# A perceiver block in fp32 on one core: the score order turned, the clip bound by way of DRAM, 76 padded first maxima

## The reference

```
x = x + xattn(layernorm(x), ctx_768, ...)   # x: (4, 256, 256), ctx_768: (4, 4096, 192)
x = x + attn(layernorm(x), ...)
x = x + ffn(layernorm(x), ...)

def xattn(query, key_value, ...):           # 16 heads of width 16
    q, k, v = query @ Wq + bq, key_value @ Wk + bk, key_value @ Wv + bv   # split into heads
    attn = clip(einsum('bhqd,bhkd->bhqk', q, k) * D ** -0.5, -10000, 10000)
    return softmax(attn) @ v @ Wo + bo
```

## Time and profile before

| | us |
|---|---|
| median of 3 runs | 1135.63 (1135.35 to 1148.06) |
| the profiled execution, whole | 1132.47 |
| its span, first to last instruction | 1130.7 |
| PE busy | 1043.2 |
| DVE busy | 825.7 |
| ACT busy | 712.5 |
| POOL busy | 380.7 |

### The profile page before, as it was taken

One profiled execution on the slowest core, in us unless ns is written; L12 is line 12 of the kernel. 1 busy time (PEld: TensorE's weight loads), 2 busy tenths in 40 slices (PEclk: granted clock), 3 DMA queues, 4 the chain that ended last, 5 costly groups with the idle time before them and its releaser, 6 DMA issues.

```text
span 1130.7 us, 29261 instructions
## 1 busy us (share of the span) xinstructions
PE 1043.2 (92%) x11521; PEld 718.0 (63%) x11521; DVE 825.7 (73%) x1549; ACT 712.5 (63%) x1382; POOL 380.7 (34%) x440
## 2 busy tenths in 40 slices
PE   7899797999999999999999999999999888978997
PEld 6687575767767676766767676655555454646655
DVE  7566686889888888888888888878878223693553
ACT  2222476777787777877877787767777654405342
POOL 5733445445444544444445442040000000203320
PEclk9899599999999999999999999979999899999999
DMA  7854653546455554555545454224431100000001
GB/s 218 236 170 136 186 167 104 173 137 169 141 165 156 145 154 144 168 148 145 167 136 162 142 162 113 61 70 117 136 99 43 30 2 2 1 1 2 3 1 38
DMA packets 117137, 128.56 MB, mean 114 GB/s; under 512 B 20007, under 2 KB 91370, under 8 KB 116970
## 3 DMA queue, kind: packets, MB, share of 16 engines
q1 hardware_dynamic: 111498, 120.20, 36.6%
q10 hardware_dynamic: 5472, 6.23, 2.1%
HBM read 88.61 MB, written 37.75 MB: 112 GB/s over the span
## 4 chain that ended last, share of the span: by engine, by line
PE 76%; issue 7%; DVE 7%; ACT 7%; DMA 1%; POOL 1%; SPq 1%; ACTq 0%; POOLq 0%; DVEq 0%
PE acc L1794 21%; PE st L1754 16%; PE mx L1740 9%; PE kps L1702 8%; PE misc L1740 5%; DVE free_k L1436 2%; PE st L1598 2%; ACT prob L994 2%; ACT qst L906 1%; PE mx L1736 1%; PE setB L2053 1%; ACT prob L1082 1%; DVE mxp L1189 1%; PE acc L1598 1%; PE mx L1593 1%
## 5 line engine op out<-in xcount | busy, mean ns | idle before, releaser
L1189 DVE TENSOR_REDUCE mxp<-mx 128x1 f32<-128x512 f32 x709 | 466.5, 683 | 106.4 <-PE mx L1740 71.3
L994 ACT ACTIVATE prob<-st 128x512 f32<-128x512 f32 x704 | 377.1, 600 | 152.7 <-PE st L1754 152.2
L1754 PE MATMUL st<-qst,kst 51*128 51x256 f32 x2048 | 409.9, 311 | 31.5 <-ACT qst L906 22.4
L1754 PEld LDWEIGHTS st<-qst,kst 51*128 51x128 f32 x2048 | 299.4, 190 | 66.9 <-ACT qst L906 25.5
L1740 PE MATMUL mx<-kst,qst 51*128 51x512 f32 x645 | 267.8, 436 | 1.8 <-DVE mxp L1189 1.5
L1189 DVE TENSOR_REDUCE mxp<-misc 128x1 f32<-128x512 f32 x315 | 215.0, 682 | 36.7 <-PE misc L1740 35.8
L994 ACT ACTIVATE xn<-st 128x512 f32<-128x512 f32 x320 | 172.2, 600 | 56.8 <-PE st L1754 56.4
L1794 PE MATMUL acc<-prob,v_raw 128*17 128x256 f32 x2816 | 193.9, 394 | 9.2 <-issue 5.4
L1740 PEld LDWEIGHTS mx<-kst,qst 51*128 51x128 f32 x645 | 122.9, 191 | 69.1 <-issue 35.9
L1740 PE MATMUL misc<-kst,qst 51*128 51x512 f32 x315 | 135.6, 430 | 0.0
L1702 PE MATMUL kps<-ctx_p,w_hi 64*128 64x256 f32 x528 | 129.2, 311 | 4.9 <-POOL ctx_p L717 4.9
(11 more groups left out here) (429 smaller groups left out, 1285.0 us busy)
## 6 DMA issues: line engine op xcount, KB each, us to landing
kst<-kscr SPq DMA_DIRECT2D x240, 128.0 KB, 2.5
kscr<-kraw SPq DMA_DIRECT2D x100, 256.0 KB, 2.7
kst<-kscr SPq DMA_DIRECT2D x240, 64.0 KB, 2.6
ctx<-in_ctxT SPq DMA_DIRECT2D x93, 128.0 KB, 2.7
ctx<-in_ctxT SPq DMA_DIRECT2D x184, 64.0 KB, 2.4
kscr<-prob SPq DMA_DIRECT2D x16, 256.0 KB, 4.6
kscr<-o_sb SPq DMA_DIRECT2D x12, 256.0 KB, 4.0
qscr<-v_raw SPq DMA_DIRECT2D x8, 256.0 KB, 2.5
```

Source lines behind the costliest of these rows:

```text
L994: act.activation(exps(unit_at(n)), st_bank("scores", unit_at(n))[:, :], ACT.Exp).then_inc(exp_done, 1)
L1189: dve.reduce_max(at, bank_of_max(n)[:, :], AX.X).then_inc(max_red, 1)
L1754: mm = pe.matmul(st_bank("scores", n)[:, h * T:(h + 1) * T], kst[row, j // 2, at:at + P], qst[row, 2 * (q % 3) + j // 2, :], start=True, s ...
```

## The change

- **The order in a step.** The step's last score, unit n+3, moves behind `values` and so to the next step's start, where its halves alternate with those of the next score. Maxima come one pass later, the fourth one ahead of three passes and of score n+1. The heads of the maxima go 0, 2, 1, 3 in place of 1, 0, 2, 3.
- **The bound** `low` is no longer made by TensorE and ScalarE in full: ScalarE takes the exponential of the 128x8 shift (`low_bound`, once a group), SP writes these 1024 numbers to DRAM and reads them back onto all partitions. The two matmuls and two activations of each group go, and their two places among the score banks.
- **The first 76 maxima** are all padded (`qz2`, in the memory of `xn`, holds group 1's queries), and three of four are followed by a piece of projection.
- **The shift** has its place among the score banks, and its copy on ScalarE, at t = 58.
- **VectorE** makes the low parts of the weights, behind its 76 reductions; GpSimd splits the first context chunk ahead of key chunk 19. VectorE's copy of the second half of a value chunk comes at t % 8 = 5, ScalarE's copies at t % 4 = 0.
- **GpSimd** adds the first output bias in four parts behind groups 1 to 4, not at once behind group 0.

```diff
-                    if more:
-                        max_unit(n + AHEAD)
-                    score_half(n, 0)
-                    score_half(n, 1)
-                    next(some, None)
...
-                    score_half(n + 3, 0)
-                    next(some, None)
-                    score_half(n + 3, 1)
-                    next(some, None)
+                    if n:
+                        score_half(n - 1, 0)
+                    score_half(n, 0)
+                    if n:
+                        score_half(n - 1, 1)
+                    score_half(n, 1)
+                    next(some, None)
                     if more:
+                        max_unit(n + AHEAD)
...
+                    for h in range(2):
+                        score_half(n + 2, h)
+                    for _ in range(2):
+                        next(some, None)
                     if more:
                         max_unit(n + 3 + AHEAD)
-                    next(some, None)
-                    next(some, None)
-                if t == 3:
-                    for e in range(2):
-                        spread_low(q, e)
+                    for _ in range(3):
+                        next(some, None)
+                    for h in range(2):
+                        score_half(n + 1, h)
...
+            def write_low(q):
+                sp.wait_ge(low_col, q + 1)
+                with nc.allow_non_contiguous_dma("1024 bounds from columns to a row"):
+                    sp.dma_start(lscr[q].rearrange("(j n p) -> p j n", j=4, n=QT), lowc[:, :, :]).then_inc(low_set, 16)
+            def read_low(q):
+                sp.wait_ge(low_set, 32 * q + 16)
+                wait(sp, clip_done, UQ * q)
+                sp.dma_start(low[:, :, :].rearrange("p j t -> p (j t)"),
+                             lscr[q].rearrange("(o n) -> o n", o=1).to_broadcast([P, 4 * T])).then_inc(low_set, 16)
...
-                act.activation(low_pairs[:, :, e, :], st_bank("low", 2 * q + e)[:, :].rearrange("p (i t) -> p i t", i=2),
-                               ACT.Exp, bias=negclip[:, :]).then_inc(low_set, 1)
+                act.activation(lowc[:, :, :], shift[:, :, :], ACT.Exp, bias=negclip[:, :],
+                               scale=-1.0).then_inc(low_col, 1)
...
-            return m - m // 6 + F0 if m % 6 < 5 else None
+            return m - m // 4 + F0 if m % 4 < 3 else None
...
+            for raw, hi, lo in weights:
+                dve.tensor_tensor(lo, raw, hi.bitcast(F32), ALU.subtract).then_inc(w_lo_set, 1)
...
-                if q == 0:
+                if 1 <= q <= 4:
                     pool.wait_ge(bo_in, 32)
-                    add_bias(0)
-                    pool.wait_ge(x_bias, 4)
+                    add_bias(0, (q - 1,))
+                    pool.wait_ge(x_bias, q)
```

More of the change, by code:

```diff
@@ L113, in build @@
         low = sb("low", [P, 4, T])
-        low_pairs = low[:, :, :].rearrange("p (i e) t -> p i e t", e=2)
         accs = sb("accs", [P, T])
@@ L382, in build @@
             st_users.append(("scores", unit_at(n)))
-            if t == 3:
-                st_users += [("low", 2 * q), ("low", 2 * q + 1)]
-            if t == 59 and q + 1 < NQ:
+            if t == 58 and q + 1 < NQ:
                 st_users.append(("shift", q + 1))
@@ L591, in _ @@
                     sp.wait_ge(st_ps, UQ * q + 8 * k + 8)
+                    if k == 7 and q + 1 < NQ:
+                        write_low(q + 1)
                     if 8 * q + k + RB < 8 * NQ:
@@ L673, in q_split, with add_bias @@
                 pool.tensor_tensor(q_sb[:, :, cols], q_sb[:, :, cols], q1[:, :, cols], ALU.subtract).then_inc(q_2, 1)
-            def add_bias(k):
+            def add_bias(k, parts=range(4)):
                 pool.wait_ge(ln_xn, NT * (k + 1))
-                for n in range(4):
+                for n in parts:
                     xs = x_sb[:, 2 * n:2 * n + 2, :]
@@ L1006, in _ @@
                         v_copy_half(c, 0)
-                if t == 60 and q + 1 < NQ:
+                if t == 57 and q + 1 < NQ:
+                    low_bound(q + 1)
+                if t == 58 and q + 1 < NQ:
                     shift_rows(q + 1)
@@ L1151, in ones_rows @@
                 for r in (32, 96):
-                    dve.memset(kst[r:r + 32, :, first * 512:end * 512].bitcast(F32), 1.0).then_inc(ones_set, 1)
+                    dve.memset(kst[r:r + 32, :, first * 512:end * 512].bitcast(F32), 1.0).then_inc(rows_set, 1)
             def norm_part(first, end):
@@ L1345, in _ @@
                     reduce_unit(n + AHEAD)
-                if t % 8 == 6 and v_job(q, t // 8) is not None:
+                if t % 8 == 5 and v_job(q, t // 8) is not None:
                     v_copy_half(v_job(q, t // 8))
@@ L1944, in _ @@
                         slot_products(at)
+            for h in range(2):
+                score_half(NU - 1, h)
             values(NQ - 1, 15)
```

124 lines of the change are left out of this document (61 added, 63 removed).

## The result

| | median of the runs | profiled run | its span | granted clock |
|---|---|---|---|---|
| before | 1139.8 us (1135.4 to 1148.1, 4 runs) | 1132.5 | 1130.7 | 0.967 |
| after | 1368.6 us (1353.5 to 1377.6, 4 runs) | 1372.3 | 1370.5 | 0.896 |

The account below looks back on a forecast made before the run. Bound: a chain through ScalarE and three score banks, not TensorE's work. Prologue -9, group 0 -2.3, groups 1 to 10 +33, 11 to 13 +5.3, 14 +2.3, 15 +0.7: together +30, 1165 us by the median's measure, range 1138 to 1192.

Parts of the forecast that it names:

- prologue: Before the first values: VectorE makes the low weights, first pass at 119.6, first values about 125; -9 us (-5 to -12).
- groups 1 to 10: Main groups: each 2.8 us longer at 53.1, plus 5 for the bias quarters; +33 us in all.
- groups 11 to 13: Late groups: from 153.0 us to 158.3, with steps of 3.16 and 2.2 a group at the seams; +5.3 us.
- The other ring: Three banks of maxima in each step: the fourth waits for the first's reduction until 1.50; step 3.16 against 2.885 us.
- the first rival: In each step the fourth maximum finds its bank free, TensorE's work bounds, steps of 2.80, 1075 us; chance 9%.
- From group to group: Seam costs over sixteen plain steps: shift 1.1, transpose 0.2, GpSimd 0.5, clock 0.3; a group 53.1 us, +2.8.
- The bias: Quarters behind groups 1 to 4 show in full, four times 1.25 us, against 5.4 saved behind group 0; nothing won.
- The bound by DRAM: Write of 1024 elements and 512 KB read, 16 times: costed at nothing, block loads late if the write took over 9 us.
- the seams gave nothing back: Rival between groups: no shift wait, no half clock, GpSimd in time, steps at 3.10; 1144 or 1136 us; chance 13%.
- no load was pulled ahead of a waiting one: Rival in each step: the held maximum's weights load during its wait, saving 0.115 us, 1138 us; chance 6%.
- Pauses of 0.2 us in each step: Rival on TensorE's clock: pauses of 0.3 to 0.5 us in each step lower it, 31 us more, 1196; chance 6%.
- the sign named for being wrong: In the main groups: value blocks 2.8 us apart, or a clock under 1.00 mid group, would refute the forecast.

Follow-up runs that it names:

- without the trip: The changed kernel with neither the write of the 1024 bounds to DRAM nor the 512 KB read back; 1194.5 us, ratio to before 1.050.
- run 7: The changed kernel without the DRAM write and read, first maximum at the step's head, fourth behind score n+1; 1146.1 us, ratio to before 1.009.
- run 9: The changed kernel without the DRAM write and read, old step order and places, bias in one piece behind group 0; 1134.0 us in one run.
- run 2: The changed kernel with the bound's DRAM write and read issued in the middle of its group; 1304.4 us, ratio to before 1.148.
- run 12: The changed kernel without the bound's DRAM write and read, SP's writes of K chunks 16 to 18 moved earlier; 1191.5 us.
- run 6: The kernel before plus an unread write per seam of 1024 four-byte elements, each 64 bytes from the next in DRAM; 1140.9 us in one run.
- run 5: The kernel before plus an unread 4 KB write per seam, 32 bytes in one piece per partition; 1139.9 us, ratio to before 1.002.

## Why the prediction was right and wrong

The span grew by 239.8 us: 174.3 by the trip, 65.5 by the rest (without the trip against before, profiled runs). The second part against the prediction's own terms (one profile against one, so the first row can be off by some 3 us and the last by 5: behind the last values all these kernels take anything from 181 to 187):

| term | forecast | without the trip |
|---|---|---|
| prologue | -9 | +6.8 (first values 140.98 against 134.15) |
| group 0 | -2.3 | -1.3 |
| groups 1 to 10 | +33 | +49.8 |
| groups 11 to 13 | +5.3 | +2.2 |
| groups 14, 15 | +3.0 | +2.9 |
| behind the last values | 0 | +5.1 |

**The other ring: right.** 1.50 for the fourth maximum, 0.67 behind it, 3.16 to 3.19 for the step: all as the trace has them, in all groups, and run 7 shows the cause. One detail was off: TensorE came to the fourth maximum about 1.36 in, not 1.04, so it is held for 0.16 and not 0.46. The forecast step doesn't depend on it, but what can be won by freeing the ring does: run 7 came to 3.00 with passes and not to the 2.80 that the first rival gave.

**From group to group: right where it was looked at, with two terms missing.** The step with the shift was forecast at 1.1 over a plain one and is 4.38, or 1.2 over. But two steps ahead of it take 3.33 and 3.92, and nothing in the forecast says so. VectorE's and GpSimd's timelines there, without the trip:

```profile
570.08 0.59 DVE L1217 TENSOR_SCALAR spad<-shift 128x8 bf16<-128x8 f32 x1
...
571.17 0.85 DVE L1220 SCALAR_TENSOR_TENSOR sres<-shift,spad 128x8 f32<-128x8 f32 x1
...
572.55 0.18 DVE L1224 SCALAR_TENSOR_TENSOR spad<-sres 128x8 bf16<-128x8 f32 x1
...
573.22 0.74 DVE L1229 TENSOR_TENSOR spad<-sres,spad 128x8 bf16<-128x8 f32 x1
```

```profile
570.01 0.61 POOL L686 CAST kraw<-kraw 128x512 fp32r<-128x512 f32 x1 [5.01 <-ACT kraw L895]
570.70 1.29 POOL L688 TENSOR_TENSOR kraw<-kraw 128x512 f32<-128x512 f32 x1
571.94 0.60 POOL L736 CAST ctx_p<-ctx 128x512 fp32r<-128x512 f32 x1
572.62 1.28 POOL L738 TENSOR_TENSOR ctx_p<-ctx,ctx_p 128x512 fp32r<-128x512 f32 x1
```

Three operations on eight columns take 0.59, 0.85 and 0.74, and each ends 0.03 to 0.06 behind the end of a GpSimd operation. The fourth starts in a gap of GpSimd's and takes 0.18. In groups 11 to 14, where GpSimd splits nothing, the three take 0.17, 0.16 and 0.18. In the kernel before only one of the four falls into a GpSimd operation and takes 0.70; the change has moved two more there. They delay the reductions behind them, and a ring bound by reductions has no cover for that. In groups 11 to 13 the second of these steps is 3.17. That is 0.9 us a group. The first and the last step of a group are 0.2 and 0.35 over forecast, which makes 54.2 for a plain group against 53.1. The quarters of the bias and the half clock behind them add some 10 us over groups 1 to 5; four times 1.25 was forecast.

**The bias: right.** Nothing won; 3 us lost in the profiles, which is within their scatter (run 9).

**The bound by DRAM: wrong, and nearly all of the miss.** "I cost it at nothing; if the write took over 9 us, block loads would come late by the rest." It took 10.3. The step that failed is that I priced the write by its bytes and by who waits for its semaphore, and not by what it does to the other transfers: block loads came late (run 2), and so did what GpSimd's branch waits for. The second half of the failure is "I count this 3.2 as fixed": GpSimd's stretch behind its branch has a packet of instructions in it and grew with the queue on the DMA engines, to 12 or 13 us. With no slack at the seam (12.5 of wait at most, 142 in all), and the clock falling during each standstill, it came to 11.6 us a group. The trace before could show the second half, the q14 packets and GpSimd's silence behind its branch. It holds no write of this layout, so the jam itself took a run to see.

**The prologue: wrong, -9 forecast, +6.8 measured.** Three terms. The last projection piece was to end 3 us later than before and did so 6.7 later (118.8 against 112.1), so VectorE had its reductions done at 122.2 instead of 118.2 (these without the trip; over all profiles the piece ends at 114.0 to 118.8 with this prologue and at 112.1 to 114.7 with the old one). The low parts of the weights took 2.8 on VectorE in place of 1.4, again beside GpSimd: the first pass came at 125.1 (119.6). And TensorE's pause of 9.7 us for the exponentials behind ScalarE's first copy wasn't seen at all: the copy waited for a write that SP issued 8 us later than before (run 12). SP is late from its wait for Q's projections on. That these come later because of the slower filling is my reading of the trace; no run changed the filling alone. I followed TensorE and VectorE through the prologue and not SP's list. Even the earliest first values of any such profile, 135.0, are 10 us behind the forecast.

**The rivals.** None held. The ring held; the seams gave nothing back; no load was pulled ahead of a waiting one. Pauses of 0.2 us in each step didn't bring the clock down: without the trip it was granted at 1.00 from 426 to 947. But the sign named for being wrong, a clock under 1.00 in the middle of groups, did appear in the changed kernel, behind the standstills: two steps of group 13 and five of group 14 took 5.0.

## What to carry to other kernels

A small transfer that nobody waits for can stop every other one: before moving a value through DRAM, lay it out so that each partition writes its bytes in one piece, or issue it only where it is needed (here inside the branch, which these inputs never take). When the chain that bounds a step is removed, look for the next ring and feed it from the step's first instruction; a first maximum that starts 0.34 us later made each of 237 steps 0.28 longer. And follow the issuing queue through a prologue as closely as the engines: it is in order, and 5 us of lateness at one wait was 8 us at its end.

## What the chip showed that I had not expected

- 1024 elements of 4 bytes, neighbours in DRAM, from 128 partitions: 10.3 us to land, and for 8 us the 16 DMA engines together move 14 GB/s (after). The same number of elements 64 bytes apart: a median of 3.2 us to land (run 6). As 32 bytes per partition: 1.4 us (run 5). Neither of these two shows in the time.
- Behind GpSimd's branch over the clip path an instruction packet comes over the DMA engines before GpSimd goes on: 3.4 us in all before, 12.1 behind the jam.
- VectorE's small operations with SBUF operands wait for GpSimd's running one (0.85 in place of 0.16), and its reductions from PSUM don't (0.68 throughout). The Trainium skill ("GPSIMD Engine Reference", section "1. Specifications") names instructions in a 2-port mode or with two SBUF inputs as the ones that contend. The operations at 571.17 and 573.22 have two inputs, and there the trace agrees and adds the price: the wait lasts to the end of GpSimd's operation. The one at 570.08 has one input and waits as well; whether it runs in a 2-port mode no view shows. Its like in the kernel before, which starts 0.03 behind the start of a GpSimd operation (at 578.07), isn't held and takes 0.17.
- TensorE's clock stays at 1.00 (the 2.4 GHz level) through pauses of 0.2 to 0.6 us in every step, and fell to 0.50 within the standstills of 9 to 12 us at the seams, 1 to 4 us after TensorE stopped, for 10 to 17 us (groups 1 to 12). It takes no long standstill: without the trip it fell at 364.2, right behind a pause of 2.2 us, for 3.4 us. And it can stay down under work, as in group 14 of the changed kernel, for 37.5 us.
